# Four graph layers on one core: index loads by turns of seven chunks, and GpSimd takes over the slot waits and the word that rows have landed

## Time and profile before

| what | value |
| --- | --- |
| median of the runs | 11011.55 us |
| lowest, highest | 11010.56, 11024.71 us |
| span of the profiled execution | 10951.1 us |
| median minus span | 60.5 us |
| GpSimd (POOL) busy | 6399.5 us, 58% |
| TensorE (PE) busy | 5958.3 us, 54% |
| DVE busy | 3019.2 us, 28% |
| ScalarE (ACT) busy | 1215.4 us, 11% |
| moved by DMA | 946.56 MB, mean 86 GB/s |

### The profile page before, as it was taken

The page is one execution under the profiler, slowest core; times in us unless marked ns, Lnnn a source line. Parts: engine busy times, 40 slices in busy tenths (PEclk is TensorE's granted clock), DMA queues, the critical chain, the costliest instruction groups (busy, mean ns, idle before and its releaser), DMA issues. The chain is left out here.

```text
span 10951.1 us, 157890 instructions
## 1 busy us (share of the span) xinstructions
PE 5958.3 (54%) x23750; PEld 4067.4 (37%) x23751; DVE 3019.2 (28%) x7227; ACT 1215.4 (11%) x2511; POOL 6399.5 (58%) x6737
## 2 busy tenths in 40 slices
PE   3666537566775667666676566643344233433344
PEld 2344436333443334333343333432334233322344
DVE  3334455212231122312232123331222122321122
ACT  1111126211110111101111111100000000000000
POOL 3655635466555656466554665546666666656665
PEclk8566669778887888878887788875666556665566
DMA  5777744233322333233332333211111111111111
GB/s 160 214 216 219 205 132 120 83 86 83 84 79 80 86 82 85 74 84 84 83 85 74 85 82 81 74 51 44 45 48 46 45 45 46 45 41 45 45 47 44
DMA packets 969624, 946.56 MB, mean 86 GB/s; under 512 B 436011, under 2 KB 703462, under 8 KB 969060
## 3 DMA queue, kind: packets, MB, share of 16 engines
q0 software_dynamic: 213248, 462.82, 16.0%
q1 hardware_dynamic: 648536, 393.32, 13.5%
q10 hardware_dynamic: 107788, 89.93, 2.5%
HBM read 799.72 MB, written 152.12 MB: 87 GB/s over the span
## 5 line engine op out<-in xcount | busy, mean ns | idle before, releaser
L742 POOL DMA_INDIRECT rows<-node_rows,idx x5488 | 5363.3, 977 | 3572.2 <-SPq L587 1916.9
L1480 DVE SCALAR_TENSOR_TENSOR onehots<-iota_f,win_base,dst_ch 128x512 f32<-128x512 f32 x1722 | 1294.3, 752 | 6499.6 <-remote 3897.1
L890 PE MATMUL ps_seg<-rows,onehots 128*128 x6864 | 1455.2, 380 | 2340.9 <-DVE sums L1500 995.2
L890 PEld LDWEIGHTS ps_seg<-rows,onehots 128*128 128x128 f32 x6864 | 1270.6, 277 | 2520.9 <-issue 2514.8
L890 PEld LDWEIGHTS ps_seg<-onehots 128*128 128x128 f32 x7840 | 1184.2, 221 | 1609.0 <-issue 917.7
L890 PE MATMUL ps_seg<-onehots 128*128 128x128 f32 x7840 | 1235.3, 308 | 936.3 <-DVE sums L1500 487.5
L969 PE MATMUL ps_big<-q_res,ident 128*128 (+1 forms) x1960 | 1270.6, 736 | 842.8 <-remote 365.2
L969 PE MATMUL ps_big<-rows,ident 128*128 (+1 forms) x1960 | 1176.8, 687 | 2.5 <-issue 2.5
L742 POOL DMA_INDIRECT sums<-kv_rows,idx x784 | 769.5, 981 | 510.2 <-SPq L587 270.8
L1188 ACT ACTIVATE onehots<-ps_big 128x512 f32<-128x512 f32 x980 | 574.5, 597 | 4382.9 <-remote 2076.7
L969 PEld LDWEIGHTS ps_big<-q_res,ident 128*128 128x128 f32 x1960 | 358.0, 227 | 918.9 <-issue 914.6
(11 more groups left out here) (205 smaller groups left out, 2572.5 us busy)
## 6 DMA issues: line engine op xcount, KB each, us to landing
q_res<-gates_by_edge SPq DMA_DIRECT2D x784, 256.0 KB
rows<-node_rows,idx POOLq DMA_INDIRECT x5488
rows<-dst_padded SPq DMA_DIRECT2D x196, 256.0 KB
value_rows_by_edge<-sums SPq DMA_DIRECT2D x196, 256.0 KB
gates_by_edge<-gate ACTq DMA_DIRECT2D x196, 256.0 KB
rows<-value_rows_by_edge SPq DMA_DIRECT2D x196, 256.0 KB, 3.1
idx<-src_padded SPq DMA_DIRECT2D x1568, 2.0 KB
node_rows<-h_res ACTq DMA_DIRECT2D x49, 448.0 KB
```

Source lines behind the costliest of these rows:

```text
L742: pool.indirect_dma_start(target[:, r, j, :], None, table, bass.IndirectOffsetOnAxis(ap=idx[:, r, j:j + 1], axis=0)).then_inc(rows_landed[ ...
L890: last = nc.tensor.matmul(banks[u % len(banks)][:, 0:width], onehots[:, u, j, :], rhs(j), start=j == 0, stop=j == J - 1)
L1480: V.scalar_tensor_tensor(onehots[:, u, :, :], of_window_.rearrange("p (a n) -> p a n", a=1).to_broadcast([P, J, P]), win_base[:, ds(w, 1)] ...
```

## The change

The index tile gets two halves of seven chunks, `idx[:, 2, RING, J]`, and SyncE loads a whole turn of seven chunks with one DMA (`load_idx`). The counter `slot_free` goes. GpSimd loads for each turn the seven steps at which the slots come free from `free_at` into registers (`load_free`), and waits itself for `read_sem`, the counter of TensorE's (in pass 0 DVE's) progress. A new counter, `pass_begun`, tells it that a pass may start. GpSimd also tells of landed rows: between the third and the fourth gather of a chunk it waits for the rows of the chunk before (in the layers for the gates too) and increments `rows_ready` (`tell_rows`). SyncE keeps the other loads (`fill`), which it now starts for seven chunks at once at the start of a pass and then as slots come free; in pass 0 it tells of a `dst` row one chunk later, and spills a chunk four chunks later (`SPILL_LAG = 4`), and GpSimd waits for a slot's spill before it gathers into it. Scores are stored two turns back instead of one. SyncE's loop body covers two turns, GpSimd's 14 chunks. In pass 1 `rows_ready` is no longer incremented, so the counts that TensorE waits for are shifted by one pass.

The core of the diff:

```diff
-        idx = sb("idx", [P, RING, J], i32)
+        idx = sb("idx", [P, 2, RING, J], i32)
-        slot_free = sem("slot_free")
+        pass_begun = sem("pass_begun")
...
+            def load_free(first, count):
+                regs = [sp.alloc_register(f"free_at{i}_{next(load_no)}") for i in range(count)]
+                sp.load(regs, free_at[0:1, ds(first, count)])
+                return [sp.snap(r, donate=True) & 255 for r in regs], regs
...
+                def load_idx(turn, half):
+                    sp.dma_start(idx[:, half, :, :], idx_by_turn[ds(table, 1), ds(turn, 1)].rearrange("t g p c j -> p (t g c) j"))\
+                        .then_inc(idx_loaded[half], 16)
...
+                def tell_dst_row(r, turn):
+                    wait_alone(sp, "sp", dst_row_landed[r], (turn + 1) * 16)
+                    sp.sem_inc(dst_row_ready, 1)
+                def spill(c, r, turn):
+                    wait_alone(sp, "sp", rows_landed[r], (turn + 1) * (16 * J))
+                    sp.dma_start(v_d[ds(c, 1)].rearrange("c p (j d) -> p (c j) d", d=D),
+                                 kv_rows[:, r, :, D:2 * D]).then_inc(spilled[r], 16)
+                def follow(turn, r):
+                    tell_dst_row((r - 1) % RING, turn if r >= 1 else turn - 1)
+                    back = r >= SPILL_LAG
+                    spill(turn * RING + (r - SPILL_LAG), (r - SPILL_LAG) % RING, turn if back else turn - 1)
...
+                if gathers:
+                    load_idx(1, 1)
+                if gathers:
+                    sp.sem_inc(pass_begun, 1)
+                for r in range(RING):
+                    fill(r, r)
...
+                def make_turn(turn, half, more=True):
+                    early = 0 if isinstance(turn, int) and turn == 1 else 1
+                    freed, regs = load_free(turn * RING - (RING + early), RING + early) if kind != "rows" else ([], [])
+                    for r in range(RING):
+                        if kind == "rows":
+                            continue
+                        wait_alone(sp, "sp", read_sem, freed[early + r] + read_base)
+                        fill(turn * RING + r, r)
+                        if kind == "scores":
+                            follow(turn, r)
+                            if r == 1 and early:
+                                wait_alone(sp, "sp", score_added, freed[0])
+                                store_scores(turn - 2)
+                    if gathers:
+                        wait_alone(sp, "sp", rows_ready, (before + turn) * RING)
+                    if gathers and more:
+                        load_idx(turn + 1, 1 - half)
...
+                def tell_rows(r, turn):
+                    if gated:
+                        wait_alone(pool, "pool", gates_landed[r], (gates_before + turn + 1) * 16)
+                    pool.wait_ge(rows_landed[r], (before + turn + 1) * (16 * J)).then_inc(rows_ready, 1)
...
+                def load_free(first):
+                    held[:] = [pool.alloc_register(f"pool_free_at{i}_{next(load_no)}") for i in range(RING)]
+                    pool.load(held, free_at[0:1, ds(first, RING)])
+                    return [pool.snap(reg, donate=True) & 255 for reg in held]
...
-                def body(c, r, turn):
-                    pool.wait_ge(idx_loaded[r], (before + turn + 1) * 16)
-                    wait_alone(pool, "pool", slot_free, before * RING + c + 1)
+                def body(c, n, pair):
+                    half, r = divmod(n, RING)
+                    turn = pair * 2 + half
+                    if r == 0:
+                        wait_alone(pool, "pool", idx_loaded[half], (pairs_before + pair + 1) * 16)
+                        if is_first(c):
+                            wait_alone(pool, "pool", pass_begun, (0 if first else k - 1) + 1)
+                        else:
+                            freed[:] = load_free(turn * RING - RING)
+                    if not (isinstance(c, int) and c < RING):
+                        wait_alone(pool, "pool", read_sem, freed[r] + read_base)
+                        if first:
+                            wait_alone(pool, "pool", spilled[r], turn * 16)
                     for j in range(J):
                         pool.indirect_dma_start(
                             target[:, r, j, :], None, table,
-                            bass.IndirectOffsetOnAxis(ap=idx[:, r, j:j + 1], axis=0)).then_inc(rows_landed[r], 16)
-                each_chunk(pool, RING, body)
+                            bass.IndirectOffsetOnAxis(ap=idx[:, half, r, j:j + 1], axis=0)).then_inc(rows_landed[r], 16)
+                        if j == J - 2 and not is_first(c):
+                            tell_rows((r - 1) % RING, turn if r >= 1 else turn - 1)
+                each_chunk(pool, 2 * RING, body)
```

98 lines of the change are left out of this document (42 added, 56 removed).

## The result

The changed kernel takes 10955.69 us (median of 8 runs, 10946.0 to 10972.38), the kernel before 11018.13 (8 runs, 10984.2 to 11052.25): ratio 0.9941, 95% interval 0.9924 to 0.9959. It is faster by 0.6%, where 9% had been forecast; 10020 us and the whole range 9150 to 10750 were wrong. The profiled execution took 10948.21 us, its span 10946.3, so that only 2 us lie around a span; the 60 us that the prediction put between span and median were the difference of one run from others.

What follows compares the result with a forecast made beforehand. The prediction took SyncE's relay to set the pace of GpSimd's gathers. Terms -165 - 400 - 420 - 20 - 15 + 30, summed there to -990, took 10951 to 9961 us, with 60 added 10020; range 9150 to 10750.

Steps and rivals of the forecast that it cites:

- The floor: Every gather pass: 784 gathers back to back at 0.977 + 0.30 us can't take less than 1001 us.
- the second paragraph: Who is late behind GpSimd's slot_free waits: SyncE, waiting 7.5 of 1267 us in the score pass, sets the pace.
- -165: Score pass: SyncE's instructions per chunk fall from 18 to 13, giving 1100 us instead of 1267.
- -400: Four layer passes: SyncE's relay, taken as 100 us a pass between 26 and 118, goes.
- -420: Three convolutions: the 141 us a pass that waiting for SyncE's word costs TensorE goes, leaving 1046 us each.
- The small terms: Value pass, slots filled seven ahead rather than five: -20 us; between passes, last chunks told sooner: -15 us.
- Rival C: DVE-TensorE exchange: relay only hid its slowness; slot waits stand at 1500 us or more; 10680 us, chance 0.22.
- (a): GpSimd's 216 loads of seven steps: 0 to 130 us; nothing in layers, 10 a convolution, 30 in all with masks.
- (b): GpSimd's in-line wait for the previous chunk's rows, ahead of the fourth gather: covered up to 5.0 us landing, taken as 0.
- rival D: GpSimd's in-line wait for landed rows binds, score pass nearest to it: slower, 11280 us, chance 0.08.
- (c): Wait for slots moves from SyncE to GpSimd: no new wait, one relay less; in scores also waits for the spill.
- (d): Edges and scores: next turn's indices asked for only when previous is consumed; taken as nothing, without cover 675 us.

Runs made afterwards that it cites:

- the version two chunks behind: Changed kernel, with rows told two chunks behind in the score pass and steps loaded one by one: 10829.72 us (0.9954 of the kernel before), again 10947.17 us (0.9957).
- one gather's shift: Changed kernel, with GpSimd waiting for and telling the previous chunk's rows behind the fourth gather, not the third: 9037.88 us, 1.0032 of the kernel before.
- the deep ones: Four-deep VectorE-TensorE exchange on the changed kernel: 10753.51 us (0.9761); with rows told two chunks behind and loads one by one: 10675.32 us (0.9805).
- the six with stops: Changed kernel, with GpSimd waiting for its own landing after every second chunk, run again on a quick chip: 11264.11 us.

## Why the prediction was wrong

**What stood.** The floor (784 gathers at 0.977 + 0.30 us) is what all eight passes of the kernel before run at on the quick chips. The counts came as written (224 index loads, no waits of TensorE for SPq L640). Rival C's test came true if the waits put to "remote" are counted: 1779 us of waits for slots, over the 1500 it named, with TensorE's name on 578. Its second sign, VectorE's "issue" growing, didn't: "remote" grew, 3897.1 to 4158.7, and "issue" fell from 1368.9 to 1111.8.

**The step that failed** is the second paragraph: SyncE "never rests, and sets the pace". It hardly waited, that was so; but it wasn't at work all that time, and the conclusion was wrong. Its instructions fill 730 of the 1267 us of the score pass, those of 0.7 us included; 354 us are the gaps without a wait told above. Without the crawl its work leaves it 336 us of waiting in a score pass of 1008. The three terms that rest on it, -165, -400 and -420, came out as +48, -22 in all four layers (5058 to 5036, the passes summed from the traces) and -28 in the three convolutions (3561 to 3533). The small terms gave about as little as they promised: the stretch with the value pass -1, the stretches between the later passes +3. The 0.36 us per instruction that I divided out was a mean over normal and crawling instructions and the gaps between them, and I scaled it by 1.2 where the right question was what makes it so long. I had the fact, "while gathers run without a break, SyncE's small instructions stretch", and VectorE's 11.16 us in the earlier trace rows; I used it to shade one term, not to ask what would be left when every engine has it.

**Rival C** was nearest to the mechanism, at 0.22 (the exchange between VectorE and TensorE is slow because of the crawl and not by itself: on a quick chip it keeps up), and it too was priced wrongly: a third of the gain was to remain, and 6% of it did (62 of 990). What I held against it, TensorE's 8.06 us for L640 in a pause of GpSimd, was only that the relay came last, not that it was what lacked. When several parties crawl together, the one that the profile names last is not the one whose removal helps.

**GpSimd's new work.** (a) The load of seven steps was priced from VectorE's row of 0.598 us for eight registers, and I said that this disagreed with the Trainium skill (Runtime: NRT & Kernel Launch, "Instruction fetch mechanics": about 200 ns per register, 1.4 us). The skill was nearer for GpSimd:

```profile
L782 POOLq TENSOR_LOAD <-free_at x216: 1005/1609/3512, 195.8 to 10871.6; - x108
```

1.6 us for seven, 0.29 for one (in the variant that loads one by one). A row from one engine doesn't price another. That it would be hidden was right for seven passes and wrong for the score pass (some 50 us on a quick chip). (b) The landing wait, taken as 0, costs 81 us in the score pass of a quick chip. The prediction took cover up to a landing of 5.0 us from rows that land after some 3; in that pass the median is 4.7 us, and 109 of the fourth gathers came late. It named that pass as nearest to the risk, and rival D's direction, slower, is what the quick kind shows, at 1.0145, though through a stall of some 0.4 us per chunk and not through a period of 6.4. (c) No trace shows a cost. (d) In the first trace GpSimd waits 14.9 us for index loads, four times in all, against nothing forecast.

**The conclusion on the change.** Removing the relay removes something that was late only by the crawl. Where there is a crawl the other engines have it as well, and the counts between them come late (0.994); where there is none, only the costs are left (1.0145).

**What stays open.** What makes some chips crawl and others not: the five chips of the experiments were three of the slow kind and two of the quick, and nothing in the traces says why. What in a gather by index slows the others. Why the counts of TensorE's sums come late and VectorE's don't. Whether the version two chunks behind brings the changed kernel level with the one before on a quick chip: it ran only on chips with the crawl, and the 51 us that were left in the score pass after one gather's shift (1058 us) are seen as idle time of GpSimd, but their removal was not tried. No version that ran on both kinds beats the kernel before on both: the deep ones lead on the slow kind (0.976 and 0.9805), the kernel before on the quick.

## What to carry to other kernels

When one party of a chain never rests, ask whether it has much to do or does it slowly: look at the longest of its small instructions and at the gaps between them, and at those of the other engines in the same stretch, before counting its removal as a gain. Look also whether a count is updated when the instruction that makes it ends. A wait moved in line on the engine that sets the pace needs room for the longest landing of its own pass, not the typical one of another. And let a second chip confirm a kernel that sits at such an edge, with a reference on the same chip: here the sign of the change depended on it. When an experiment adds work, look in its trace whether the work is there.

## What the runs showed of the hardware

- On three chips the kernel before took 10882 to 11006 us in the experiments, on two others 9006 and 9013, the same program each time. On one chip the runs of a kernel agreed within about 0.6%, but for one of 12155 us among the six with stops that have the median of 11264.
- On the former, from some 8 us into an unbroken run of GpSimd's gathers by index, many register instructions of TensorE, VectorE and SyncE take about 0.7 us (428 of 2117 of TensorE's in the changed kernel's convolutions). Means over the convolutions of the first trace: 75, 64 and 212 ns, against 40, 49 and 70 on a quick chip. Those of ScalarE and GpSimd keep their 54 and 36 ns.
- There the count of a finished sum of TensorE also reaches VectorE late: over 1 us late 231 times, 1340 us in three convolutions, the longest 19.4 us. On a quick chip it was 3 times and 4 us, in the kernel before. Of VectorE's counts to TensorE one was.
- The profile itself holds fewer records there: 1612 updates of the count of TensorE's sums for 1960 sums, against 1933 on a quick chip, of the same kernel.
- Direct transfers of as many bytes, read in order, don't do it, neither from SyncE's queue nor from GpSimd's, and stops of 2.6 us after every 8 gathers all but end it.
- GpSimd's part in a plain copy of 128 rows of 512 bytes is 0.535 us (busy 1256.89 us for 2352), in a gather by index of as many bytes 0.98.
- The granted clock of TensorE was 0.81 in the kernel before's first layer with the crawl and 0.91 without, both means over stretches at its two levels of 1.2 and 2.4 GHz; the matmuls of that layer were busy 829 and 770 us.
